# A one-core LSTM on Trainium2: products of x for two steps at a time in a bank of their own, and the output gates' adds on GpSimd

## What is computed

```python
xW = jnp.einsum('ntd,dg->ntg', x, Wx) + b
def step(carry, xw_t):
    prev_h, prev_c = carry
    a = xw_t + prev_h @ Wh
    i = jax.nn.sigmoid(a[:, :Hdim])
    f = jax.nn.sigmoid(a[:, Hdim:2 * Hdim])
    o = jax.nn.sigmoid(a[:, 2 * Hdim:3 * Hdim])
    g = jnp.tanh(a[:, 3 * Hdim:])
    next_c = f * prev_c + i * g
    next_h = o * jnp.tanh(next_c)
    return ((next_h, next_c), next_h)
c0 = jnp.zeros_like(h0)
_, hs = jax.lax.scan(step, (h0, c0), jnp.swapaxes(xW, 0, 1))
return x + jnp.swapaxes(hs, 0, 1)
```

## Time and profile before

| | us |
|---|---|
| median of 3 runs | 1928.33 (1927.99 to 1928.96) |
| the profiled execution | 1931.45 |
| its span, first to last instruction | 1929.7 |
| first step's first transpose | 51.4 |
| last step's second transpose | 1924.8 |

### The profile page before, as it was taken

The page is one execution under the profiler, slowest core; times in us unless marked ns, Lnnn a source line. Parts: engine busy times, 40 slices in busy tenths (PEclk is TensorE's granted clock), DMA queues, the critical chain, the costliest instruction groups (busy, mean ns, idle before and its releaser), DMA issues.

```text
span 1929.7 us, 145599 instructions
## 1 busy us (share of the span) xinstructions
PE 1878.0 (97%) x65588; PEld 1621.7 (84%) x65588; DVE 1819.2 (94%) x9739; ACT 991.1 (51%) x4241; POOL 2.6 (0%) x14
## 2 busy tenths in 40 slices
PE   1999999999999999999999999999999999999998
PEld 1888888888888888888888888888888888888887
DVE  8999999999999999999999999999999999999998
ACT  4455554555554555555555545555555555555554
POOL 0000000000000000000000000000000000000000
PEclk9999999999999999999999999999999999999999
DMA  5000000000000000000000000000000000000000
GB/s 202 15 27 21 22 27 21 21 24 24 21 22 27 21 21 27 22 21 21 27 21 22 27 21 21 23 25 21 22 27 21 21 24 24 22 21 27 18 13 15
DMA packets 39216, 51.56 MB, mean 27 GB/s; under 512 B 4416, under 2 KB 36160, under 8 KB 38592
## 3 DMA queue, kind: packets, MB, share of 16 engines
q1 hardware_dynamic: 37152, 37.77, 6.0%
q10 hardware_dynamic: 1440, 4.49, 0.6%
HBM read 25.46 MB, written 16.78 MB: 22 GB/s over the span
## 4 chain that ended last, share of the span: by engine, by line
PE 90%; DVE 7%; ACT 1%; DMA 1%; issue 0%; ACTq 0%; DVEq 0%
PE acc L261 44%; PE acc L267 23%; PE acc L273 23%; DVE turned L449 1%; DMA wh<-in_wh 1%; ACT x_halves L183 1%; DVE products L466 1%; DVE o_gate L471 0%; DVE preact L458 0%; DVE h_halves L491 0%; ACT acc L202 0%; DVE h_halves L482 0%; DVE wx_low L351 0%; DVE gates L476 0%; DVE wh_low L351 0%
## 5 line engine op out<-in xcount | busy, mean ns | idle before, releaser
L261 PE MATMUL acc<-wx_high,x_halves 128*32 128x256 f16 x16384 | 932.5, 273 | 5.2 <-ACT acc L202 1.8
L261 PE MATMUL acc<-wx_low,x_halves 128*32 128x256 f16 x16384 | 932.6, 273 | 0.6 <-issue 0.3
L273 PE MATMUL acc<-wh_high,h_halves 128*32 128x256 f16 x16384 | 724.7, 275 | 0.0
L267 PE MATMUL acc<-wh_low,h_halves 128*32 128x256 f16 x16384 | 720.9, 274 | 2.4 <-DVE wh_low L351 2.4
L216 ACT ACTIVATE gates<-preact 128x96 f32<-128x96 f32 x1024 | 289.3, 283 | 769.2 <-DVE preact L458 594.0
L449 DVE STREAM_TRANSPOSE turned<-acc 128x256 f32<-128x256 f32 x1024 | 457.0, 446 | 62.3 <-PE acc L273 56.3
L267 PEld LDWEIGHTS acc<-wh_low,h_halves 128*32 128x32 f16 x16384 | 389.8, 96 | 96.5 <-DVE h_halves L482 79.8
L261 PEld LDWEIGHTS acc<-wx_high,x_halves 128*32 128x32 f16 x16384 | 442.9, 97 | 24.8 <-ACT acc L202 11.4
L273 PEld LDWEIGHTS acc<-wh_high,h_halves 128*32 128x32 f16 x16384 | 354.7, 96 | 123.4
L261 PEld LDWEIGHTS acc<-wx_low,x_halves 128*32 128x32 f16 x16384 | 442.9, 97 | 12.3 <-issue 2.3
L202 ACT ACTIVATE acc<-b_rows 128x256 f32<-128x256 f32 x1024 | 345.3, 369 | 0.9 <-issue 0.3
(11 more groups left out here) (62 smaller groups left out, 390.3 us busy)
## 6 DMA issues: line engine op xcount, KB each, us to landing
out<-out_ring SPq DMA_DIRECT2D x128, 128.0 KB, 1.7
x_ring<-in_x SPq DMA_DIRECT2D x120, 128.0 KB, 2.2
wx<-in_wx ACTq DMA_DIRECT2D x4, 512.0 KB, 8.1
wx<-in_wx SPq DMA_DIRECT2D x4, 512.0 KB, 8.1
wh<-in_wh SPq DMA_DIRECT2D x4, 512.0 KB, 16.8
wh<-in_wh ACTq DMA_DIRECT2D x4, 512.0 KB, 17.2
x_ring<-in_x SPq DMA_DIRECT2D x2, 512.0 KB, 16.9
b_rows<-in_b ACTq DMA_DIRECT2D x1, 256.0 KB, 21.5
```

Source lines behind the costliest of these rows:

```text
L261: pe.matmul(acc[par][n][32 * j:32 * j + 32, 0:GL], x_halves[:, slot, c], w[:, c, n * Q + j], start=False, stop=False, skip_group_check=True)
L267: pe.matmul(acc[par][n][32 * j:32 * j + 32, 0:GL], h_halves[1 - par][:, c, 0:2], w_low["wh"][:, c, n * Q + j], start=False, stop=False, sk ...
L273: last = pe.matmul(acc[par][n][32 * j:32 * j + 32, 0:GL], h_halves[1 - par][:, c, 1:3], w_high["wh"][:, c, n * Q + j], start=False, stop=c ...
```

## The change

1. **Products of x.** A matmul's stationary operand now holds the 16 batch rows of two steps (a pair) of one half, not two halves of one step. Three products are made (high x with `w_high`, low x with `w_high`, high x with `w_low`), each over 512 columns, both groups at once: 48 matmuls of 512 columns for two steps instead of 128 of 256. The low with low product is left out. They accumulate in banks of their own, `x_acc[pair % 2]`, half of them in each step.
2. **Mask.** A step's share is copied from `x_acc` to `acc` by ACT (`fill`, one ACTIVATE of 512 columns from PSUM to PSUM), with `step_mask` as the scale of each partition: 1 on the 16 rows of the step's parity, 0 on the other 16. The bias is placed once for a pair (`place_bias`, 512 columns).
3. **Output gates.** POOL adds the halves of the output gate of both groups (`preact[n][:, 6:8]`), each after `turned_ready`; DVE's `add_all(0)` becomes `add_three(0)` and `add_last(1)` goes. Both `last_gate` on ACT wait for POOL.
4. **Order.** On DVE `output_gate(0)` stands ahead of `new_cell(0)`. The work for the next chunk's scale is two steps earlier and a step shorter (acc_scale and scales share step 9), x's parts are made in steps 11 to 15 for a whole chunk, and `x_sums` is in step 6.
5. **Layout.** x comes as pairs of steps; the output row reads it with a stride.

```diff
-            def place_bias(t):
-                for n in range(NG):
-                    act.activation(acc[t % 2][n][:, 0:GL], b_rows[:, n], ACT.Copy, scale=b_scale[t // CHUNK % 2])\
-                        .then_inc(bias_placed, 1)
+            def place_bias(pair):
+                act.activation(x_acc[pair % 2][:], b_rows[:], ACT.Copy, scale=b_scale[2 * pair // CHUNK % 2]).then_inc(bias_placed, 1)
+
+            def fill(t):
+                act.activation(acc[t % 2][:, :, 0:GL], x_acc[t // 2 % 2][:], ACT.Copy, scale=step_mask[:, t % 2:t % 2 + 1])\
+                    .then_inc(acc_filled, 1)
...
             for t in range(T):
                 par = t % 2
                 chunk, at = divmod(t, CHUNK)
+                if t % 2 == 1 and t + 3 < T:
+                    act.wait_ge(acc_filled, t + 1)
+                    place_bias((t + 3) // 2)
                 if t + 1 < T:
-                    place_bias(t + 1)
+                    if t % 2 == 1:
+                        act.wait_ge(x_summed, (t + 1) // 2 + 1)
+                    fill(t + 1)
...
                 def last_gate(n):
-                    if n == 1:
-                        act.wait_ge(o_preact_ready, t + 1)
+                    act.wait_ge(o_preact_ready[n], t + 1)
...
-            def input_part(slot, par, n):
-                for c in range(C):
-                    for w in (w_high["wx"], w_low["wx"]):
+            def input_part(pair, of):
+                for c in of:
+                    for half, w in ((0, w_high["wx"]), (1, w_high["wx"]), (0, w_low["wx"])):
                         for j in range(Q):
-                            pe.matmul(acc[par][n][32 * j:32 * j + 32, 0:GL], x_halves[:, slot, c], w[:, c, n * Q + j],
-                                      start=False, stop=False, skip_group_check=True)
+                            last = pe.matmul(x_acc[pair % 2][32 * j:32 * j + 32], x_halves[:, pair % (CHUNK // 2), c, half],
+                                             w[:, c].rearrange("p (n q) g -> p q n g", q=Q)[:, j],
+                                             start=False, stop=False, skip_group_check=True)
+                return last
...
+                    elif t % 2 == 1:
+                        if at == 13:
+                            pe.wait_ge(x_ready, QUARTERS * (chunk + 1) + 1)
+                        pe.wait_ge(bias_placed, pair + 1)
+                        input_part(pair, (0,))
+                        pe.wait_ge(acc_filled, t + 2)
+                        input_part(pair, (1,))
+                    else:
+                        input_part(pair, (2,))
+                        pe.wait_ge(acc_filled, t + 2)
+                        input_part(pair, (3,)).then_inc(x_summed, 1)
...
+            for t in range(T):
+                for n in range(NG):
+                    pool.wait_ge(turned_ready, NG * t + n + 1)
+                    pool.tensor_tensor(preact[n][:, 6:8], turned[n][:, 6:8, 0, :], turned[n][:, 6:8, 1, :], ALU.add)\
+                        .then_inc(o_preact_ready[n], 1)
...
                 turn(0)
-                add_all(0)
+                add_three(0)
                 turn(1)
                 gate_products(0)
                 add_three(1)
+                output_gate(0)
                 new_cell(0)
-                output_gate(0)
-                add_last(1)
                 gate_products(1)
```

More of the change, by code:

```diff
@@ L120, in lstm_kernel @@
         gates_ready = sem("gates_ready")
-        o_preact_ready = sem("o_preact_ready")
+        o_preact_ready = [sem(f"o_preact_ready{n}") for n in range(NG)]
         o_ready = sem("o_ready")
@@ L147, in _ @@
                 if chunk + 2 < CHUNKS:
-                    sp.dma_start(x_ring[chunk % 2][:, at:at + QUARTER], x[:, first + 2 * CHUNK:first + 2 * CHUNK + QUARTER, :])\
+                    ahead = first // 2 + CHUNK
+                    sp.dma_start(x_ring[chunk % 2][:, at // 2:at // 2 + QUARTER // 2], x[:, ahead:ahead + QUARTER // 2, :])\
                         .then_inc(x_loaded[chunk % 2], 16)
@@ L162, in _ @@
                 pool.memset(out_ring[half][:], 0.0).then_inc(out_free[half], 1)
+            for parity in range(2):
+                pool.memset(step_mask[:, parity:parity + 1], parity).then_inc(mask_cleared, 1)
+            pool.wait_ge(mask_cleared, 2)
+            for j in range(Q):
+                for parity in range(2):
+                    pool.memset(step_mask[32 * j:32 * j + B, parity:parity + 1], 1 - parity).then_inc(mask_ready, 1)
+            pool.wait_ge(mask_ready, 2 * Q)
+            for half in range(2):
+                pool.wait_ge(out_free[half], 1)
+            for t in range(T):
[3 more added lines that the diff above has]
+                        .then_inc(o_preact_ready[n], 1)
         @block.scalar
@@ L281, in _ @@
                     for j in range(Q):
-                        opened = pe.matmul(acc[p][n][32 * j:32 * j + 32, 0:GL], h_halves[0][:, 0, 0:2], w_high["wx"][:, 0, j],
+                        opened = pe.matmul(acc[p][32 * j:32 * j + 32, n, 0:GL], h_halves[0][:, 0, 0:2], w_high["wx"][:, 0, j],
                                            start=True, stop=False, skip_group_check=True)
                     opened.then_inc(acc_opened, 1)
-            pe.wait_ge(x_ready, 1)
-            for n in range(NG):
-                pe.wait_ge(bias_placed, n + 1)
-                input_part(0, 0, n)
+            for i in range(2):
+                for j in range(Q):
+                    opened = pe.matmul(x_acc[i][32 * j:32 * j + 32], h_halves[0][:, 0, 0:2],
+                                       w_high["wx"][:, 0].rearrange("p (n q) g -> p q n g", q=Q)[:, j],
+                                       start=True, stop=False, skip_group_check=True)
+                opened.then_inc(acc_opened, 1)
+            pe.wait_ge(x_ready, 1)
+            pe.wait_ge(bias_placed, 1)
+            input_part(0, (0, 1, 2, 3)).then_inc(x_summed, 1)
+            pe.wait_ge(bias_placed, 2)
+            input_part(1, (0, 1))
+            pe.wait_ge(acc_filled, 1)
             pe.wait_ge(h_ready, NG)
@@ L448, in turn @@
                     dve.wait_ge(acc_ready, nth[n])
-                    dve.transpose(turned[n][:].rearrange("p g s b -> p (g s b)"), acc[par][n][:, 0:GL]).then_inc(turned_ready, 1)
+                    dve.transpose(turned[n][:].rearrange("p g s b -> p (g s b)"), acc[par][:, n, 0:GL]).then_inc(turned_ready, 1)
                 def add_three(n):
```

105 lines of the change are left out of this document (52 added, 53 removed).

## The result

The changed kernel takes 1959.46 us (median of 4 runs, 1959.41 to 1959.56) against 1928.57 (1927.99 to 1928.96) before: a ratio of 1.0156, 95% interval 1.0144 to 1.0168. It is slower, where 1915 was forecast and a gain was held more likely than a loss; the time lies inside the range of 1908 to 1973, near what the second rival gives. The profiled execution took 1959.49 us, its span is 1957.7.

A forecast was written before the change was run, and what follows sets the result against it. It took a latency loop through DVE and ACT as the bound, not PE. Narrower add less reorder gained 7.7 us, chunk work 5.8, others 0: 13.5 us in sum, giving 1915 us, range 1908 to 1973.

The forecast's parts named there:

- second rival: GpSimd's read of `turned[1]` holds up DVE by D: 1915 + 511 x D, 1941 to 2007, middle 1971 us; chance 31%.
- PE is not the bound: PE waits for h twice a step, so 0.45 us less x matmuls gains 0; rival PE bound: 1700 us, 2%.
- Bias and mask are covered: On ACT: `fill` 0.5 to 0.8 us, bias 0.35 to 0.65, 0 on the path; without cover 6 us in all.
- Narrower add of group 0: On DVE: 96 columns instead of 128, 0.25 for 0.29 us, a gain of 0.04 us a step.
- The reorder gives back 0.025: `output_gate(0)` ahead of `new_cell(0)` on DVE: gives back 0.03 of 0.04, leaving some 0.015 us a step, 7.7 us gained.
- ends at 1.96: ACT's tanh of group 0's cell, after the reorder, starts at 1.75 us of the step and ends at 1.96.
- latency hidden: GpSimd's output gate adds, 0.13 to 0.18 us, up to 0.3: group 0's has 0.65 us of room, so latency is hidden.
- what POOL does to DVE: I take 0: Cost to DVE of GpSimd's adds: taken as 0, with bounds 0 and one whole add, 0.18 us a step.
- not late: Rival: GpSimd's first add ends after 1.1 us, `output_gate(0)` blocks `new_cell(0)`; 0.1 a step, 1966 us; chance 6%.
- the gap in front of `gate_products(1)`: Rival: GpSimd comes in only there, holding `gate_products(1)` up by some 0.07 us: 1935 us, with less about 1928; chance 12%.
- The clock: Rival: PE's clock falls to 1.2 GHz at times, the 0.45 us tail 0.3 longer; in all steps over 2060; 2%.
- Chunk work: Per chunk, 31 times: step 14 gains 0.14 us, `x_sums` load 0.1, step 9 loses 0.05; net 5.8 us gained.

The follow-up runs named there:

- e2: The changed kernel with all adds back on DVE in the old order and GpSimd idle: 1924.0 us.
- e14: e2 with eight more matmuls of 512 columns in each step, into a bank that nothing reads: 1926.2 us.
- e3: The changed kernel with GpSimd adding group 0's output gate alone, DVE adding group 1's, and `new_cell(0)` ahead of `output_gate(0)`: 1906.8 us.
- e1: The changed kernel with the reorder undone, `new_cell(0)` ahead of `output_gate(0)` again: 1938.9 us.
- e7: e1 with GpSimd's add for group 1 waiting for DVE's add of group 1 and not for the transpose: 1906.5 us.
- e5: e2 with an idle GpSimd memset of 32 columns of a spare tile in each step, released by the transpose of group 1: 1923.2 us.
- e6: e2 with an idle GpSimd add of two 32-column pieces of a constant tile in each step, released by the transpose of group 1: 1923.3 us.
- e9: e6 with one of GpSimd's two waits gone, so its add starts 0.08 and not 0.14 us behind the transpose of group 1: 1956.4 us.
- e11: e2 with every x matmul of 512 columns written as two of 256, 224 PE instructions a step: 1923.5 us.

## Why the prediction was wrong, point by point

- **PE is not the bound; the loop through DVE and ACT is: right.** e2 shows it with the x part, the mask and the chunk work alone changed (1924.0), e14 with PE made as long as before (1926.2).
- **Bias and mask are covered: right.** `fill` takes 0.64 us and the bias 0.58, inside the ranges, and no step waits for them.
- **Narrower add of group 0, 0.04 a step: right in kind, 0.034 in size.** e3 against e2: 17.2 / 511. DVE's add is 0.26, not 0.25; GpSimd reads beside it, and no run has the narrow add without that.
- **The reorder gives back 0.025 (0.03 rounded): mis-sized.** It gives back 0.040 (e1), more than the 0.034 won. The step that failed is "ends at 1.96": a tanh that no other stands in front of takes 0.23 us and not the 0.21 that I took from the earlier trace rows, where it queues. In the trace of before the first tanh of a cell takes 0.213 us and the second 0.229 in the median, after the change both take 0.229: these 0.016 us are what was missing. No run has the reorder without the stretched add.
- **GpSimd: latency hidden, right; "what POOL does to DVE: I take 0", wrong.** This is the step that decided. It costs 0.063 a step (e1 against e7, 32.4 / 511), inside the bounds 0 and 0.18 that I had written down. I took 0 because ACT and DVE show no stretch side by side; that says nothing of GpSimd, and no row showed it reading beside DVE. Since 0.025 was enough to turn the sign, a term without a row behind it should not have been put at nothing. The add itself takes GpSimd 0.25 us alone and up to 0.35 beside DVE, more than the 0.13 to 0.18 of the nearest rows.
- **The second rival was the case.** Its formula gives 1915 + 511 x 0.063 = 1947; with the reorder's missing 0.015, 1955; the rest, some 4 us, is the narrower add (17.5 us gained for 20.4) and the chunk work (4.6 for 5.8). The terms as measured close: 1928.6 - 4.6 (e2) - 17.5 (e7) + 32.4 (e1) + 20.6 = 1959.5.
- **The other rivals were not the case.** GpSimd's first add ends at 0.85 us of the step and ACT has the output gate at 1.18, ahead of `output_gate(0)` at 1.47: not late. In the gap in front of `gate_products(1)` an add costs nothing: e7 puts one there, and the products start at 1.83 and at 1.84 in e3, which has none there. The clock was granted at 0.998 to 1.0 in every run. That rival gave PE 0.4 us of idle time a step before and 0.9 after; these are gaps of the weight loads, PE itself was busy for 997.66 of 1000 us before and waits 0.45 us a step after.
- **Chunk work: right.** Step 14 is plain now (0.13 us less), the `x_sums` step too (0.07 less), step 9 is 3.760, 0.043 longer. Times 31 that is some 5 us, and e2 lies 4.6 under the kernel before by the medians; 5.8 was reckoned. By the spans it is 7.5, since the profile of the kernel before has six steps of about 4.0 us, 2.5 us in all, that belong to no term of the sum.

The Trainium skill's page SBUF — State Buffer, section Who interferes with whom, has the rule that came true: two SBUF inputs on DVE and a read by GpSimd contend, a write alone does not (e5), and who comes second waits (e6, e9). It calls what they share an exclusive lock and says, of DVE's 2-port modes, that the one that issues first has it for the whole instruction. For these two adds the trace differs: GpSimd's 0.25 us began 0.06 ahead, and the add was held up by 0.06, not by 0.19. The Trainium skill's page GPSIMD Engine Reference, section 3.1, Elementwise — side-by-side cycle accounting, gives about 2.6 cycles an element for a two-input add and reckons with 1.2 GHz: an estimate of 32 x 2.6 / 1.2 = 69 ns for this one, near the hold-up of 62 ns; so it may be the reading alone that blocks. No run here settles that.

## What to carry to other kernels

Before work is moved to GpSimd, look at what DVE does in the same 0.3 us: beside a transpose from PSUM, a wait, or an instruction that has time to spare it is free or nearly so (e3, e7, e6), ahead of a two-input instruction on the critical loop it cost 0.06 us each time. An engine that is 97% busy can be off the path: read what its loads wait for, and ask what the loop is. Of instructions in a loop bound by latency, order them by whose result is waited for longest; `output_gate(0)`, whose result is used late, ahead of `new_cell(0)`, whose result is not, cost 20 us.

## What was not expected of the hardware

- Which instruction of DVE pays depends on 0.06 us of start time of GpSimd's (0.08 or 0.14 us behind its release): the add of group 1 (0.32 for 0.25) or the next one with two inputs (0.24 for 0.18).
- A GpSimd copy of 32 columns that began 0.07 us ahead held DVE's add up by about 0.01 us, a two-input add of as many, begun 0.05 ahead, by 0.06.
- PE kept up with 224 matmuls and weight loads in a step of 3.65 us in every run of e11 (within 1 us), and with 256 did not: single steps 0.3 to 0.4 us longer, 44 to 137 of 512 in three traces, with runs 8 to 22 us apart. In the first comparison the same 256 went with 6 such steps and runs 1 us apart. The late loads stand 1.2 to 1.6 us behind the landing of a 16 KB packet of instructions. It hits the kernel before and not the changed one, so PE's smaller number of instructions, worth nothing on the path, is worth a steady time.
